# Softmax attention: the second pair of score matmuls between the two halves of the weighted values

## The chip, the cores and the metric

The kernel runs on one core of one Trainium2 chip. The metric is the device time of one execution in microseconds (us); the median over repeated runs counts. The engines are TensorE (PE; PEld is its weight load), VectorE (DVE), ScalarE (ACT), GpSimd (POOL) and SyncE (SP).

## The reference, cut to what matters

Two decoder layers over x of 16 sequences x 128 tokens x 128 features. Layer 0 is a self attention, a cross attention over ctx_1024 and a butterfly feed-forward; layer 1 is a linear attention, an autocorrelation attention and a mixture of experts. The change touches only the two softmax attentions of layer 0, both with 16 heads of 8 features:

```python
q = (x @ Wq).reshape(n, s, H, DH)
k = (x @ Wk).reshape(n, s, H, DH)
v = (x @ Wv).reshape(n, s, H, DH)
attn = jnp.einsum('nqhd,nkhd->nqkh', q, k) * scale
attn = jax.nn.softmax(attn, axis=-2)
z = jnp.einsum('nqkh,nkhd->nqhd', attn, v).reshape(n, s, d)
z = jnp.einsum('nqd,de->nqe', z, Wout)
return x + z
```

The cross attention is the same with the queries from x, keys and values straight from ctx_1024, and a bias on the output.

## The kernel before, in words

`attention` (L149) runs both attentions in one software pipeline of 32 passes, one pass for one sequence of one attention: passes 0 to 15 are the self attention, 16 to 31 the cross attention. The 16 heads of a sequence are four groups of four. Each engine has its own program; there is no scheduler: the order of an engine's instructions is the order of the code, and semaphores join the engines.

For one sequence the work is: first scores in bf16 (L569, one matmul of 512 columns per group, its four heads side by side), the negated row maximum of each head by VectorE (L473, one reduction per group), the maxima spread as a first term into a PSUM bank (L582, four matmuls per group) and the exact scores in fp32 added to it (L588), the exponential by ScalarE (L413, one per group), the weighted values in fp32 with a column of ones that gives the denominator (L608, 16 matmuls with an output of 32 partitions each, which are 32 matmul instructions in the trace, since the trace shows two for each of these fp32 matmuls), a copy out of PSUM by ScalarE (L419), transposes back (L620), division by VectorE (L479, L481), a transpose (L612), again the copy L419, the output projection (L624) and the residual (L490).

TensorE's loop (L640 to L652) works on several sequences at once. In pass i it does, in this order: the exact scores of sequence i (`shifted_scores`); the weighted values of sequence i-1 and the transpose of the divided output of i-2 (`values`); the first scores of groups 2 and 3 of sequence i+1 (`scores(i + 1, 1)`); the maxima of i+1 for groups 0 and 1; the transposes and the projection of `mix`; in 14 of the passes 1 to 30 (1 to 10, 13, 17, 21 and 25) a round of projections or transposes for a coming group of four sequences (`fill`, L545 to L554); the maxima for groups 2 and 3; the first scores of groups 0 and 1 of i+2.

What ties this order to other engines:

- The first scores use two banks for four groups, so those of groups 2 and 3 wait until VectorE has read groups 0 and 1 (`maxed`, L567).
- The maxima of group g of sequence i+1 wait for two things: the exponential of group g of sequence i, which frees the bank (`exped`, L578), and the reduction of group g of i+1 (`maxed`, L579).
- ScalarE's order in a pass is the exponentials of groups 0 and 1, `copy_mix` (L419), the exponentials of groups 2 and 3 (L441 to L446). `copy_mix` waits for `pv_done`, which `values` raises on its last instruction (L614); `mix` waits for `copy_mix` (L617).

Of the kernel before, what the change touches and what calls it, by code (L numbers as in the profile page):

```python
# [22 lines left out]
T = 128  # L23
D = 128
EPS = 1e-5
G, J = 4, 4
# [108 lines left out]
Q = 4  # L135
K_SLOTS = 3
GROUPS = B // Q
# [4 lines left out]
def bf16_head(ap):  # L142

    *lead, n = ap.shape
    wide = ap.bitcast(BF16)
    return wide[(slice(None),) * len(lead) + (slice(1, 2 * n, 2),)]


def attention(core, m, f, lin, a):  # L149
# [26 lines left out]
    bank_t, bank_s, bank_o, bank_r = core.bank[0:4], core.bank[4:6], core.bank[6], core.bank[7]  # L176
    scale = float(DH) ** -0.5
    SELF, CROSS = range(GROUPS), range(GROUPS, 2 * GROUPS)
# [10 lines left out]
    done_after = {kg: r + 1 for r, kg in enumerate(rounds)}  # L189

    def round_bank(r):
        return (bank_r, *bank_t[0:3])[r] if r < Q else bank_r
# [14 lines left out]
    def queries(s, g):  # L207
        return m.q[rows(g), s // Q % 2, s % Q, :]

    def keys(s, g):  # L210
        return m.k_j[rows(g), s % K_SLOTS, :, :] if s < B else m.k_ctx[rows(g), s - B, :, :]

    with nc.Block() as block:
# [321 lines left out]
        @block.tensor  # L535
        def _(pe):
            def fill(r):
                kind, g = rounds[r]
                bank = round_bank(r)
                if kind == "n" or g in CROSS:  # L540
                    if r >= Q:
                        pe.wait_ge(copied, 1 if r == Q else r)
                    pe.wait_ge(normed, Q * (g + 1))
                    for i in range(Q):
                        mm = pe.transpose(bank[:, i * T:(i + 1) * T], m.n[:, g % 2, i, :], core.ident[:, :])  # L545
                else:
                    pe.wait_ge(copied, r if r > Q else 1)
                    if kind == "v":
                        for i in range(Q):
                            mm = pe.matmul(bank[:, i * D:(i + 1) * D], m.nT[:, i * T:(i + 1) * T], m.wv[:, :],  # L550
                                           start=True, stop=True)
                    else:
                        mm = pe.matmul(bank[:, :], (m.wk if kind == "k" else m.wq)[:, :], m.nT[:, :],
                                       start=True, stop=True)  # L554
                mm.then_inc(filled, 1)

            def scores(s, pair):
                if s >= V:
                    return
                if pair == 0:  # L560
                    pe.wait_ge(copied, done_after["q", s // Q])
                    if s < B:
                        pe.wait_ge(k_made, s + 1)
                    elif s == B:
                        pe.wait_ge(k_ctx_in, 16)
                if s or pair:
                    pe.wait_ge(maxed, G * s + 2 * pair)  # L567
                for g in (2 * pair, 2 * pair + 1):
                    pe.matmul(bank_s[g % 2][:, :], bf16_head(queries(s, g)),  # L569
                              bf16_head(keys(s, g).rearrange("p j t -> p (j t)")), start=True, stop=True)\  # L570
                        .then_inc(scored, 1)

            def maxima(s, groups):
                if s >= V:
                    return
                for g in groups:
                    if s:
                        pe.wait_ge(exped, G * (s - 1) + g + 1)  # L578
                    pe.wait_ge(maxed, G * s + g + 1)  # L579
                    for j in range(J):  # L580
                        h = J * g + j
                        pe.matmul(bank_t[g][:, j * T:(j + 1) * T], m.nmax[:, h:h + 1].to_broadcast([T, T]),  # L582
                                  core.ident_b[:, :], start=(j == 0), stop=False, skip_group_check=True)

            def shifted_scores(s):
                for j in range(J):
                    for g in range(G):
                        mm = pe.matmul(bank_t[g][:, j * T:(j + 1) * T], keys(s, g)[:, j, :], queries(s, g),  # L588
                                       start=False, stop=(j == J - 1), skip_group_check=True)
                        if j == J - 1:  # L590
                            mm.then_inc(shifted, 1)

            def values(i):
                if i >= 2:
                    pe.wait_ge(o_done, i - 1)
                if i >= 3:
                    pe.wait_ge(x_done, i - 2)
                s = i - 1
                if s < V:
                    g = s // Q  # L600
                    pe.wait_ge(exped, G * (s + 1))
                    if s % Q == 0:
                        pe.wait_ge(*((copied, done_after["v", g]) if g in SELF else (v_made, g - GROUPS + 1)))
                    for half in range(2):
                        for odd in range(2):
                            for c in range(4):
                                h = 8 * half + 2 * c + odd
                                mm = pe.matmul(bank_o[32 * c:32 * c + 32, half * T:half * T + T],  # L608
                                               m.v[:, g % 2, s % Q, h, :], m.p[:, s % 2, h, :],
                                               start=(odd == 0), stop=(odd == 1), skip_group_check=True)  # L610
                if i >= 2:
                    mm = pe.transpose(bank_o[:, 2 * T:3 * T], m.o[:, :, :].rearrange("p h d -> p (h d)"),  # L612
                                      core.ident[:, :])
                mm.then_inc(pv_done, 1)  # L614

            def mix(i):
                pe.wait_ge(mix_copied, i)  # L617
                if i - 1 < V:
                    for half in range(2):
                        mm = pe.transpose(bank_o[:, half * T:half * T + T], m.mix[:, half, :], core.ident[:, :])  # L620
                if i >= 2:
                    if i == 2:
                        pe.wait_ge(out_in, 32)
                    mm = pe.matmul(bank_o[:, 2 * T:3 * T], m.mix[:, 2, :], m.w_out[(i - 2) // B][:, :],  # L624
                                   start=True, stop=True)
                mm.then_inc(mixed, 1)

            pe.wait_ge(ident_in, 16)
            fill(0)
            pe.wait_ge(proj_in, 48)  # L630
            for r in range(1, Q):
                fill(r)
            scores(0, 0)
            fill(Q)
            scores(0, 1)
            pe.wait_ge(copied, Q)
            pe.wait_ge(made, 4)
            maxima(0, range(G))
            scores(1, 0)
            for i in range(V + 2):  # L640
                if i < V:
                    shifted_scores(i)
                if i >= 1:
                    values(i)
                scores(i + 1, 1)
                maxima(i + 1, (0, 1))
                if i >= 1:
                    mix(i)
                if i in round_at:
                    fill(round_at[i])  # L650
                maxima(i + 1, (2, 3))
                scores(i + 2, 0)  # L652
# [1450 lines left out]
```

## Time and profile before

| what | value |
|---|---|
| time, median of 3 runs | 612.64 us (612.61, 612.64, 618.45) |
| the profiled execution's own time | 617.73 us |
| its span, first to last instruction | 615.6 us |
| mean granted clock of TensorE over the span | 0.875 |
| the 32 passes: first exact scores of pass 0 to those of pass 31 | 22.36 to 175.38 us |

The profile is of one execution. All durations come from it. In rows of a timeline the columns are the start in us, the duration in us from the first start to the last end of the instructions that the row merges, the engine, the line, the operation, the tiles written and read, the shapes and the count; idle time of the engine before it stands in brackets with what ended it.

### The profile page before, as it was taken

How to read it: one execution, taken by the hardware profiler on the slowest of the kernel's cores; microseconds unless marked ns; L12 is line 12 of the kernel's file. 1: busy time of each engine (PE TensorE's matmuls, PEld its weight loads, DVE VectorE, ACT ScalarE, POOL GpSimd, SP SyncE). 2: the span in 40 equal slices, each digit the busy share in tenths (PEclk: the TensorE clock that was granted, in tenths of full speed). 3: DMA queues.
4: the chain of work that ended last, by engine and by line, in shares of the span. 5: the costliest groups of instructions: out<-in, count | busy, mean ns of one | idle time of the engine just before them, and what ended most of it. 6: DMA issues, size and time to landing. Idle time of an engine off the chain costs nothing. (4 is left out here: it accounts for less than half of the span.)

```text
span 615.6 us, 13186 instructions
## 1 busy us (share of the span) xinstructions
PE 485.4 (79%) x4975; PEld 383.4 (62%) x4975; DVE 345.1 (56%) x934; ACT 239.0 (39%) x514; POOL 209.2 (34%) x234
## 2 busy tenths in 40 slices
PE   3879999999977979999999997996275232399960
PEld 1567777777754767888888886875155221266640
DVE  6546777777653446667766764344783767211114
ACT  3756666666542325444543541221121000132313
POOL 3546777799132233000000002123621000447750
PEclk9799999999996989999999997997585555599995
DMA  8960312200000011000000001200006000324417
GB/s 234 394 260 4 113 64 73 68 4 2 4 1 1 0 36 44 1 0 0 0 0 0 0 0 25 63 17 0 1 7 199 1 0 0 94 63 126 121 33 205
DMA packets 31460, 34.71 MB, mean 56 GB/s; under 512 B 5561, under 2 KB 25078, under 8 KB 31288
## 3 DMA queue, kind: packets, MB, share of 16 engines
q1 hardware_dynamic: 29208, 29.50, 15.3%
q0 software_dynamic: 2064, 4.60, 2.3%
q8 instruction: 31, 0.51, 0.4%
q14 instruction: 13, 0.11, 0.1%
q10 hardware_dynamic: 144, 0.00, 0.0%
HBM read 28.65 MB, written 5.46 MB: 55 GB/s over the span
## 5 line engine op out<-in xcount | busy, mean ns | idle before, releaser
L473 DVE TENSOR_REDUCE at_nmax<-bank 128x4 bf16<-128x512 f32 x128 | 82.5, 686 | 48.1 <-PE bank L569 48.1
L413 ACT ACTIVATE at_p<-bank 128x512 f32<-128x512 f32 x128 | 69.3, 597 | 38.2 <-PE bank L588 38.2
L95 POOL TENSOR_TENSOR var<-var,eps 128x12 f32<-128x12 f32 (+1 forms) x8 | 1.7, 206 | 191.1 <-DVE var L88 191.1
L1869 POOL DMA_INDIRECT mo_rows<-mo_n_rows,mo_src_row x24 | 23.0, 959 | 71.2 <-POOLq L1577 64.2
L582 PE MATMUL bank<-ident_b,at_nmax 128*128 128x128 bf16 x512 | 42.9, 222 | 3.9 <-DVE at_nmax L473 3.4
L582 PEld LDWEIGHTS bank<-ident_b,at_nmax 128*128 128x128 bf16 x512 | 31.0, 98 | 18.8 <-issue 9.5
L608 PE MATMUL bank<-at_p,at_v 128*32 128x128 f32 x1024 | 35.0, 276 | 3.9 <-issue 3.0
L1942 ACT ACTIVATE mo_h<-bank,mo_b 128x308 f32<-128x308 f32 x32 | 16.5, 517 | 47.1 <-PE bank L1905 47.1
L1913 PE MATMUL bank<-mo_w,mo_h 128*128 128x128 f32 (+1 forms) x192 | 32.9, 294 | 1.3 <-ACT mo_h L1942 1.3
L1040 PE MATMUL bank<-li_phi_q,li_phi_k 128*128 128x256 f32 x128 | 31.9, 393 | 0.9 <-DVE li_phi_q L908 0.9
L1051 PEld LDWEIGHTS bank<-li_v,li_am 128*128 128x128 f32 x256 | 29.8, 192 | 3.7 <-DVE li_am L915 3.1
L1051 PE MATMUL bank<-li_v,li_am 128*128 128x65 f32 x256 | 31.7, 277 | 0.1
L1913 PEld LDWEIGHTS bank<-mo_w,mo_h 128*128 128x128 f32 (+1 forms) x192 | 24.0, 172 | 11.9 <-ACT mo_h L1942 5.3
L608 PEld LDWEIGHTS bank<-at_p,at_v 128*32 128x32 f32 x1024 | 26.2, 110 | 8.1 <-issue 3.3
L1961 DVE COPY mo_xT<-bank 128x308 f32<-128x308 f32 x8 | 3.8, 478 | 48.2 <-PE bank L1896 48.2
L1637 PE MATMUL bank<-ro_reached,ro_ones_b 128*128 128x56 bf16 x160 | 10.9, 228 | 24.0 <-DVE ro_reached L1733 24.0
L1877 POOL DMA_INDIRECT mo_planes<-mo_y,mo_dst_row x24 | 23.7, 986 | 16.9 <-DVE mo_y L1968 10.5
L282 POOL TENSOR_TENSOR at_k_j<-at_kT,at_mask 128x512 f32<-128x512 f32 x16 | 16.6, 1039 | 30.7 <-PE bank L588 27.5
L1040 PEld LDWEIGHTS bank<-li_phi_q,li_phi_k 128*128 128x128 f32 x128 | 23.0, 190 | 4.3 <-DVE li_phi_q L908 1.1
L1002 ACT ACTIVATE li_tanh<-bank,li_gate_bias 128x128 f32<-128x128 f32 x64 | 18.2, 367 | 19.2 <-PE bank L1018 19.1
L989 ACT ACTIVATE li_clip_k<-bank 128x512 f32<-128x512 f32 x16 | 9.6, 597 | 40.3 <-PE bank L1018 40.3
L1637 PEld LDWEIGHTS bank<-ro_reached,ro_ones_b 128*128 128x128 bf16 x160 | 8.2, 121 | 26.7 <-DVE ro_reached L1733 25.4
(279 smaller groups left out, 1214.5 us busy)
## 6 DMA issues: line engine op xcount, KB each, us to landing
fo_w<-in_up_stages SPq DMA_DIRECT2D x9, 512.0 KB, 9.3
fo_w<-in_down_stages SPq DMA_DIRECT2D x9, 512.0 KB, 4.7
at_k_ctx<-in_ctx_heads SPq DMA_DIRECT2D x1, 4096.0 KB, 21.5
mo_w<-in_L_ffn_W SPq DMA_DIRECT2D x16, 256.0 KB, 3.1
mo_planes<-ro_zeros POOLq DMA_DIRECT2D x1, 2048.0 KB, 9.1
mo_got<-mo_planes SPq DMA_DIRECT2D x8, 256.0 KB, 4.8
x<-in_x SPq DMA_DIRECT2D x4, 256.0 KB, 3.5
au_ctx<-in_ctx SPq DMA_DIRECT2D x4, 256.0 KB, 4.0
```

Of the source, the lines that this page charges most:

```text
L282: pool.tensor_tensor(m.k_j[:, s % K_SLOTS, :, :], over(m.kT[:, g % 2, s % Q, :], J), m.mask[:, :].unsqueeze(2).to_broadcast([D, J, T]), AL ...
L413: act.activation(m.p[:, s % 2, J * g:J * g + J, :], bank_t[g][:, :].rearrange("p (j t) -> p j t", j=J), ACT.Exp, scale=scale).then_inc(exp ...
L473: dve.tensor_reduce(m.nmax[:, J * g:J * g + J], bank_s[g % 2][:, :].rearrange("p (j t) -> p j t", j=J), AX.X, ALU.max, negate=True).then_i ...
L582: pe.matmul(bank_t[g][:, j * T:(j + 1) * T], m.nmax[:, h:h + 1].to_broadcast([T, T]), core.ident_b[:, :], start=(j == 0), stop=False, skip ...
L608: mm = pe.matmul(bank_o[32 * c:32 * c + 32, half * T:half * T + T], m.v[:, g % 2, s % Q, h, :], m.p[:, s % 2, h, :], start=(odd == 0), sto ...
L1002: ins = act.activation(tanh[:, c, :], bank_g[:, c * T:(c + 1) * T], ACT.Tanh, bias=m.gate_bias[:, c:c + 1], scale=0.5)
L1040: mm = pe.matmul(bank_a[c // 2][:, 256 * (c % 2):256 * (c % 2) + 256], phi_k[:, c, :], phi_q[:, c, :, :].rearrange("p r t -> p (r t)"), st ...
L1051: mm = pe.matmul(bank_num[h // half][:, i * V1:(i + 1) * V1], am[:, h, :], v[:, h, :], start=True, stop=True)
L1637: mm = pe.matmul(bank_c[:, 0:TRIALS * E6], ones_b[:, :], reached[:, b, :, :].rearrange("t j e -> t (j e)"), start=(b == 0), stop=(b == B - 1))
L1869: pool.indirect_dma_start(out=rows[0:m, e % 2, r, :], out_offset=None, in_=n_rows, in_offset=bass.IndirectOffsetOnAxis(ap=src_row[0:m, til ...
L1877: pool.indirect_dma_start(out=planes, out_offset=bass.IndirectOffsetOnAxis(ap=dst_row[0:m, tile:tile + 1], axis=0), in_=y[0:m, e % 2, r, : ...
L1913: mm = pe.matmul(bank_y[r][0:m, 0:D], h[:, c, at[r]:at[r] + m], w2[:, par, c, :], start=(c == 0), stop=(c == CH6 - 1))
```

## The change

`values` takes a second argument and does one half of its matmuls per call; the two waits for the buffers, the wait for the exponentials and the wait for the values stand before the first half, the transpose and `pv_done` behind the second. In the loop the first scores of groups 2 and 3 stand between the two calls. Lines below `values` move down by one to five (L608 becomes L609, L612 L615, L620 L623, L624 L627). The other engines' programs keep their instructions and their order.

```diff
-            def values(i):
-                if i >= 2:
-                    pe.wait_ge(o_done, i - 1)
...
+            def values(i, half):
+                if half == 0:
+                    if i >= 2:
+                        pe.wait_ge(o_done, i - 1)
...
-                    for half in range(2):
-                        for odd in range(2):
...
+                    for odd in range(2):
+                        for c in range(4):
+                            h = 8 * half + 2 * c + odd
+                            mm = pe.matmul(bank_o[32 * c:32 * c + 32, half * T:half * T + T],
+                                           m.v[:, g % 2, s % Q, h, :], m.p[:, s % 2, h, :],
+                                           start=(odd == 0), stop=(odd == 1), skip_group_check=True)
+                if half == 0:
+                    return
...
                 if i >= 1:
-                    values(i)
+                    values(i, 0)
                 scores(i + 1, 1)
+                if i >= 1:
+                    values(i, 1)
                 maxima(i + 1, (0, 1))
```

TensorE in a pass of the cross attention without a fill, from the exact scores to the transposes of `mix`, before (at_v and at_p are values and exponentials, at_k_ctx and at_q keys and queries, at_nmax the negated maxima, at_o the divided output, at_mix what `copy_mix` wrote):

```order
L588 MATMUL bank<-at_q,at_k_ctx 128x128 x16
L608 MATMUL bank<-at_p,at_v 32x128 [waits at_exped,at_x_done,at_o_done]
L608 MATMUL bank<-at_p,at_v 32x128 x15
L612 MATMUL bank<-ident,at_o 128x128
L569 MATMUL bank<-at_k_ctx,at_q 128x512 [waits at_maxed]
L569 MATMUL bank<-at_k_ctx,at_q 128x512
L582 MATMUL bank<-ident_b,at_nmax 128x128 [waits at_maxed,at_exped]
...
L620 MATMUL bank<-ident,at_mix 128x128 [waits at_mix_copied]
```

and the same place now:

```order
L588 MATMUL bank<-at_q,at_k_ctx 128x128 x16
L609 MATMUL bank<-at_p,at_v 32x128 [waits at_exped,at_x_done,at_o_done]
L609 MATMUL bank<-at_p,at_v 32x128 x7
L569 MATMUL bank<-at_k_ctx,at_q 128x512 [waits at_maxed]
L569 MATMUL bank<-at_k_ctx,at_q 128x512
L609 MATMUL bank<-at_p,at_v 32x128 x8
L615 MATMUL bank<-ident,at_o 128x128
L582 MATMUL bank<-ident_b,at_nmax 128x128 [waits at_maxed,at_exped]
...
L623 MATMUL bank<-ident,at_mix 128x128 [waits at_mix_copied]
```

The two score matmuls, with their wait for at_maxed, moved up past the transpose and eight of the matmuls of the values; the transpose, on which `pv_done` hangs, now stands behind them.

ScalarE in the same passes, which has the same rows before and now (at_p the exponentials, at_mix the copy):

```order
L413 ACTIVATE at_p<-bank 128x512 [waits at_pv_done,at_shifted]
L413 ACTIVATE at_p<-bank 128x512 [waits at_shifted]
L419 ACTIVATE at_mix<-bank 128x384 [waits at_pv_done]
L413 ACTIVATE at_p<-bank 128x512 [waits at_shifted] x2
L385 ACTIVATE at_n<-x,at_shift,rstd 128x128
```

Nothing moved here: the copy still stands between the second and the third exponential.

## Rows read from the trace of the kernel before

**Rows 1.** The page's first part: busy time of each engine over the span.

```profile
PE 485.4 (79%) x4975; PEld 383.4 (62%) x4975; DVE 345.1 (56%) x934; ACT 239.0 (39%) x514; POOL 209.2 (34%) x234
```

**Rows 2.** Waits in 105 to 163 us: waiter, releaser, us in total, times, longest.

```profile
ACT at_p L413 <- PE bank L588: 18.8, 13, 1.9
...
PE bank L582 <- DVE at_nmax L473: 2.1, 10, 0.2
```

**Rows 3.** Timeline of pass 16, a pass without a fill.

```profile
105.17 1.27 PE L588 MATMUL bank<-at_q,at_k_ctx 32*128 32x128 f32 x32
105.59 1.29 DVE L473 TENSOR_REDUCE at_nmax<-bank 128x4 bf16<-128x512 f32 x2 [0.21 <-PE bank L569]
...
106.38 1.08 PE L608 MATMUL bank<-at_p,at_v 128*32 128x128 f32 x32
106.48 1.09 ACT L413 ACTIVATE at_p<-bank 128x512 f32<-128x512 f32 x2 [1.56 <-PE bank L588]
...
107.39 0.33 PE L612 MATMUL bank<-ident,at_o 128*128 128x128 f32 x1
...
107.65 0.40 PE L569 MATMUL bank<-at_k_ctx,at_q 32*128 32x512 bf16 x2
107.76 0.49 ACT L419 ACTIVATE at_mix<-bank 128x384 f32<-128x384 f32 x1 [0.19 <-PE bank L612]
...
107.98 0.62 PE L582 MATMUL bank<-ident_b,at_nmax 128*128 128x128 bf16 x8
108.08 1.29 DVE L473 TENSOR_REDUCE at_nmax<-bank 128x4 bf16<-128x512 f32 x2 [1.00 <-PE bank L569]
108.14 1.08 ACT L413 ACTIVATE at_p<-bank 128x512 f32<-128x512 f32 x2
...
108.44 0.39 PE L620 MATMUL bank<-ident,at_mix 128*128 128x128 f32 x2
...
109.52 0.38 PE L582 MATMUL bank<-ident_b,at_nmax 128*128 128x128 bf16 x4 [0.21 <-DVE at_nmax L473]
...
109.78 0.28 DVE L490 TENSOR_TENSOR x<-bank,x 128x128 f32<-128x128 f32 x1
...
109.85 1.27 PE L588 MATMUL bank<-at_q,at_k_ctx 32*128 32x128 f32 x32
```

**Rows 4.** Groups by line: the mean duration of one values matmul is the second number.

```profile
L608 PE MATMUL bank<-at_p,at_v 128*32 128x128 f32 x1024 | 35.0, 276 | 3.9 <-issue 3.0
```

**Rows 5.** Timeline of pass 9, a pass with a fill.

```profile
74.72 0.39 PE L620 MATMUL bank<-ident,at_mix 128*128 128x128 f32 x2
...
75.17 1.02 PE L553 MATMUL bank<-at_nT,at_wq 128*128 128x512 f32 x2
...
76.04 0.61 PE L582 MATMUL bank<-ident_b,at_nmax 128*128 128x128 bf16 x8
```

**Rows 6.** Timeline of pass 31, where the transposes of mix wait for the copy.

```profile
177.86 0.49 ACT L419 ACTIVATE at_mix<-bank 128x384 f32<-128x384 f32 x1 [0.20 <-PE bank L612]
...
178.40 0.44 PE L620 MATMUL bank<-ident,at_mix 128*128 128x128 f32 x2 [0.58 <-ACT at_mix L419]
...
178.68 0.39 PE L624 MATMUL bank<-at_w_out,at_mix 128*128 128x128 f32 x2
```

**Rows 7.** Timeline of pass 15, where VectorE has variances before the reductions.

```profile
100.43 0.28 DVE L490 TENSOR_TENSOR x<-bank,x 128x128 f32<-128x128 f32 x1
...
101.31 1.28 DVE L473 TENSOR_REDUCE at_nmax<-bank 128x4 bf16<-128x512 f32 x2
```

**Rows 8.** Timeline of pass 3: TensorE stands still inside the values.

```profile
43.35 0.42 PE L608 MATMUL bank<-at_p,at_v 128*32 128x128 f32 x6 [3.00 <-issue]
```

**Rows 9.** Stretches: length, busy us and count of PE, PEld, DVE, ACT, POOL; granted clock; DMA.

```profile
39.00:44.00 5.00, 2.00 (x49) 1.29 (x41) 1.00 (x3) 1.08 (x2) 3.75 (x5) 1.00 0.65 230
...
105.17:175.38 70.21, 67.64 (x1348) 53.83 (x1347) 51.96 (x128) 43.50 (x87) 45.14 (x31) 1.00 0.07 18
```

More of the change, by code:

```diff
@@ L591, in shifted_scores @@
                             mm.then_inc(shifted, 1)
-            def values(i):
-                if i >= 2:
-                    pe.wait_ge(o_done, i - 1)
-                if i >= 3:
-                    pe.wait_ge(x_done, i - 2)
+            def values(i, half):
+                if half == 0:
+                    if i >= 2:
+                        pe.wait_ge(o_done, i - 1)
+                    if i >= 3:
+                        pe.wait_ge(x_done, i - 2)
                 s = i - 1
@@ L600, in values @@
                     g = s // Q
-                    pe.wait_ge(exped, G * (s + 1))
-                    if s % Q == 0:
-                        pe.wait_ge(*((copied, done_after["v", g]) if g in SELF else (v_made, g - GROUPS + 1)))
-                    for half in range(2):
-                        for odd in range(2):
[L606 to L610, printed above, removed]
+                    if half == 0:
+                        pe.wait_ge(exped, G * (s + 1))
+                        if s % Q == 0:
+                            pe.wait_ge(*((copied, done_after["v", g]) if g in SELF else (v_made, g - GROUPS + 1)))
+                    for odd in range(2):
[4 more added lines that the diff above has]
+                                           start=(odd == 0), stop=(odd == 1), skip_group_check=True)
+                if half == 0:
+                    return
                 if i >= 2:
```

## The prediction

> **What bounds the kernel now.** The page's first part comes first: TensorE is busy for 79% of the span, VectorE 56%, ScalarE 39% [rows 1]. That share mixes seven stages, so the stretch that the change touches is read alone, in the waits of the cross attention and then in the timeline of one pass. The waits [rows 2] show TensorE stopped by VectorE's reductions ten times in 13 passes, 0.2 us each, 2.1 us together: once in each of the ten passes without a fill. ScalarE waits much longer for the exact scores (18.8 us), but that only says that it has time to spare somewhere in the pass; where it has none must be seen in the timeline.
>
> The reader should lay rows 3 out by engine. One pass runs from the exact scores at 105.17 to the next at 109.85, 4.68 us, and TensorE fills it but for one hole of 0.21 us, before the maxima of group 3 at 109.52. Those need two things: the last reduction, which ends at 108.08 + 1.29 = 109.37, and the last exponential, which ends at 108.14 + 1.08 = 109.22. VectorE is the later one by 0.15 us. But ScalarE ends almost as late, and for a reason of its own: after its first two exponentials it runs the copy of the mix, in order, and the copy waits for the transpose L612, which ends at 107.39 + 0.33 = 107.72; it starts at 107.76, and the last two exponentials, whose scores have lain ready since 105.17 + 1.27 = 106.44, run behind it. So there are two loops through TensorE of nearly one length: first scores of groups 2 and 3 → reductions → maxima of group 3, and values → transpose L612 → copy → two exponentials → maxima of group 3. The change shortens the first and lengthens the second.
>
> **The change part by part.** It adds no arithmetic. It moves two matmuls and their wait, per pass, past the transpose and half of the values, in passes 1 to 30 (pass 0 has no values, pass 31 no next sequence).
>
> *The first scores come earlier.* They start at 107.65 now. The values start at 106.38 and take 1.08: 32 instructions of 276 ns each [rows 4], in eight sets of four side by side, so (1.08 - 0.30)/7 = 0.11 from set to set, taking 0.30 for the first; half of them is 0.30 + 3 x 0.11 = 0.63. What follows another kind of matmul starts 0.07 before that one's end (107.39 against 107.46, 107.65 against 107.72, 107.98 against 108.05 [rows 3]). So the scores could start 0.56 after the values, at 106.94. Their wait is for the reductions of groups 0 and 1, which end at 105.59 + 1.29 = 106.88, so it costs 0 to 0.1 us; I take 0, since the margin is 0.06 and a release with a single wait took 0.05 (below). The reductions of groups 2 and 3 then end about 0.7 us earlier than now, and the hole of 0.21 us goes.
>
> *The transpose comes later.* The scores hold TensorE 0.33 us (107.65 to 107.98), and the second half pays its own start and end: values start + 0.56 + 0.33 + 0.56 = 1.45 against 107.39 - 106.38 = 1.01 now. The transpose is late by 0.44, and with it the copy (107.76 → 108.20) and the last two exponentials (ending 109.22 → 109.66). TensorE's own total hardly moves: now it goes values, transpose, scores, maxima, with three changes of the matmul's kind; afterwards values, scores, values, transpose, maxima, again three, since transpose and maxima are both 128 x 128.
>
> *Passes without a fill, 16 of 30.* The maxima of group 3 have to wait for the last exponential. From copy to L620 a release with a single wait took 177.86 + 0.49 = 178.35 to 178.40, 0.05 us [rows 6]. As things are, ScalarE would release them at 109.22 + 0.05 = 109.27, 0.25 before they start. Of the 0.44 that is added, 0.25 is therefore paid by the vanished hole, and 0.19 remains; I take 0.22, since the order of two waits in one place can cost some hundredths more. 16 x 0.22 = 3.5 us.
>
> *Passes with a fill, 14 of 30.* Here the fill stands between the transposes of mix and the second maxima [rows 5]: 75.17 to 76.04 is 0.87 us in which both reductions and exponentials end, so there is no hole to win. But the transposes L620 stand in front of the fill and wait for the copy. Now the copy ends at 108.25 and L620 starts at 108.44 without a wait; afterwards the copy ends at 108.69, L620 starts at 108.74, 0.30 later. After such a wait the next matmuls came 178.68 - 178.40 = 0.28 later [rows 6] instead of 108.66 - 108.44 = 0.22, which the rows of pass 9 bear out in sum: 75.17 - 74.72 = 0.45 for L620 and L624 together. So 0.30 + 0.06 = 0.36, rounded up by the drift above to 0.37: 14 x 0.37 = 5.2 us. Nothing covers it, since everything behind it on TensorE is queued in order.
>
> *Two passes with variances ahead of the reductions.* VectorE finishes the residual and then computes variances before the first reductions of the next pass; in pass 15 the reductions start 101.31 - 100.43 = 0.88 after the residual [rows 7], against 105.59 + 4.68 - 109.78 = 0.49 in rows 3, and they end 0.39 later in the pass. That hid behind the values before; now the moved scores wait for it in full view, and the transpose behind them. The longer pass takes about 0.1 off. 2 x 0.3 = 0.6 us (passes 15 and 19).
>
> *The start.* In pass 3 TensorE stands still for 3.00 us with nothing to wait for in the program [rows 8], while the DMA share is 0.65 [rows 9]. If that stall ends with the DMA traffic and not so long after its beginning, what passes 1 and 2 lose is hidden by it. Bounds 0 and -1.1 (three passes); I take -0.8, two passes of 0.37 and a bit of the third.
>
> *Sum:* 3.5 + 5.2 + 0.6 - 0.8 = +8.5 us. The profiled execution took 617.73 us, 2.1 more than its span of 615.6; it would become 626.2. It lies 5.1 us above the median of 612.64, and the three runs themselves differ by that much, so the change is put on the median: 612.64 + 8.5 = 621.1 us, 1.4% slower. A measurement of this kernel can tell about 1% from no change, here 6 us.
>
> **A rule to weigh.** Rows 3 show that TensorE starts a matmul of another shape only when the one before it is nearly done. The Trainium skill, "TensorEngine Tiling (Array Packing)", Key Properties, says that changing the tiling mode, and not just the tile, drains the array. The trace agrees for the pairs that it has (0.07 us before the end, three times); it has no first scores behind values. By the rule the moved scores cannot run beside the values, and the delay of 0.44 stands; without it they could run beside the second half, which is the second rival below.
>
> **The rivals.**
>
> 1. *The wait on the copy doesn't bind.* If the copy came back in time for L620, the fill passes would lose nothing and the gain or loss would be that of the other passes: 612.64 + 3.5 + 0.6 = 616.7. For it: now L620 has 108.44 - 108.25 = 0.19 of margin. Against it: the transpose is 0.44 late, more than twice that. It decides where the transpose is less than about 0.15 late.
> 2. *Faster: the scores run beside the second half of the values.* Exact scores do start 0.01 to 0.02 us behind first scores, since both use 32 rows of the array. If the values let the scores in beside them, the transpose would hardly move, the hole would go, and the maxima of group 3 would follow the last exponential: 16 x 0.25 = 4.0 us won, 608.6. Against it: every change of shape in rows 3 costs its 0.33 or 0.20 in order. It turns into a gain from the point where the transpose is late by less than 0.15 to 0.2.
> 3. *The scores themselves wait.* If the release of the moved scores takes as long as that of the maxima does now (109.37 to 109.52, 0.15), they start at 107.03, 0.09 late, in every pass, and if the reductions of groups 0 and 1 are pushed back as well, by up to 0.2: 30 x 0.09 to 0.2 = 2.7 to 6 us more, 623.8 to 627.1. For it: the margin is only 0.06. Against it: VectorE's residual ends at 110.06 in rows 3 while the next reductions wait for their scores until 110.27.
> 4. *The clock.* More holes in TensorE could lower its granted clock. Against it: in 39 to 44 us it was busy for 2.00 of 5.00 us and the clock stayed at 1.00, the 2.4 GHz level, as in the cross attention [rows 9]. At half of that the passes would cost over 100 us.
>
> **How the numbers follow.** Forecast (+5 to +11): 0.70. Rival 1: 0.12. Rival 2: 0.05. Rival 3: 0.11. Rival 4: 0.01, and 0.01 that something else wins. Slower by over 1% (above 618.8) are rivals 3 and 4 and about nine tenths of the forecast, 0.75; within 1% are rival 1, over half of rival 2 (0.03) and the rest of the forecast, 0.22; faster by over 1% (below 606.5) the other 0.02 of rival 2, if it wins more than its price, and the 0.01, 0.03. For the range I go down to 615, which takes in most of rival 1 and a start that hides all of its 1.1, and up to 628, rival 3 or one of the longer executions that the runs of before also show.
>
> **What would show it.** In the profile after: passes without a fill of about 4.90 us instead of 4.68 and those with a fill longer by 0.37; the hole before the maxima of group 3 put down to ScalarE's exponentials instead of the reductions; a new hole of about 0.3 us before the transposes of mix, put down to the copy; VectorE's second wait in the pass (1.00) much shorter; ScalarE's wait for the transpose (0.19) at 0.6 or more. The prediction is wrong if the copy starts less than 0.2 us later behind the values' start than now, if the passes with a fill keep their length, or if the hole before group 3 goes and nothing takes its place.

## The result, and the profile after

The changed kernel takes 622.95 us (median of 17 runs, 618.87 to 628.78), the kernel before 614.06 us in the 17 runs beside it. The ratio is 1.012, with a 95% interval of 1.0088 to 1.0152: slower by 1.2%. The ratio leaves out one disturbed run of the changed kernel (628.78 us) and equals the quotient of the means of the others (622.76 and 615.37 us, 7.4 us apart); the medians lie 8.9 us apart. Forecast was 1.4%, 621.1 us. The profiled execution has a span of 622.2 us, against 615.6 us before.

The page's first part after, to lay beside [rows 1], and the group of the values, beside [rows 4]:

```profile
PE 492.5 (79%) x4975; PEld 382.2 (61%) x4975; DVE 347.8 (56%) x934; ACT 239.1 (38%) x514; POOL 209.1 (34%) x234
...
L609 PE MATMUL bank<-at_p,at_v 128*32 128x128 f32 x1024 | 40.8, 278 | 0.9 <-DVE x L490 0.9
```

Only TensorE's busy time has moved much, by 7.1 us, with the same instructions. Most of it is the values: 40.8 us instead of 35.0, since two runs of 0.64 us stand in a pass for one of 1.08. Whether that is the loss, or only where it can be seen, the page can't tell.

The same pass as [rows 3], pass 16, in the timeline of the changed kernel:

```profile
107.17 1.27 PE L588 MATMUL bank<-at_q,at_k_ctx 32*128 32x128 f32 x32
107.58 1.29 DVE L473 TENSOR_REDUCE at_nmax<-bank 128x4 bf16<-128x512 f32 x2 [0.26 <-PE bank L569]
...
108.37 0.64 PE L609 MATMUL bank<-at_p,at_v 128*32 128x128 f32 x16
...
108.95 0.40 PE L569 MATMUL bank<-at_k_ctx,at_q 32*128 32x512 bf16 x2
...
109.28 0.65 PE L609 MATMUL bank<-at_p,at_v 128*32 128x128 f32 x16
109.38 1.29 DVE L473 TENSOR_REDUCE at_nmax<-bank 128x4 bf16<-128x512 f32 x2 [0.31 <-PE bank L569]
...
109.85 0.33 PE L615 MATMUL bank<-ident,at_o 128*128 128x128 f32 x1
...
110.01 0.61 PE L582 MATMUL bank<-ident_b,at_nmax 128*128 128x128 bf16 x8
110.22 0.49 ACT L419 ACTIVATE at_mix<-bank 128x384 f32<-128x384 f32 x1 [0.66 <-PE bank L615]
110.60 1.08 ACT L413 ACTIVATE at_p<-bank 128x512 f32<-128x512 f32 x2
110.76 0.20 PEld L623 LDWEIGHTS bank<-ident,at_mix 128*128 128x128 f32 x2 [0.31 <-ACT at_mix L419]
...
111.73 0.23 PEld L582 LDWEIGHTS bank<-ident_b,at_nmax 128*128 128x128 bf16 x4 [0.26 <-ACT at_p L413]
...
112.08 1.27 PE L588 MATMUL bank<-at_q,at_k_ctx 32*128 32x128 f32 x32
```

Read from the start of the values at 108.37. VectorE got what it was meant to get: its second pair of reductions starts 1.01 us after the values (109.38), not 1.70 (108.08 - 106.38 in [rows 3]), and its wait fell from 1.00 to 0.31 us. But the transpose starts 1.48 us after them instead of 1.01, and the copy 1.85 instead of 1.38. The last exponential now ends at 110.60 + 1.08 = 111.68 and the weights for the maxima of group 3 follow at 111.73, released by ScalarE. Ahead of them stands a new wait, 0.31 us, of the mix on the copy. The pass is 4.92 us long (112.08 - 107.17 = 4.91 in these rounded rows) instead of 4.68.

The waits, over 105 to 163 us as in [rows 2]:

```profile
ACT at_mix L419 <- PE bank L615: 8.5, 12, 1.0
...
PEld bank L623 <- ACT at_mix L419: 3.7, 12, 0.3
...
PEld bank L569 <- DVE at_nmax L473: 2.5, 11, 0.5
PEld bank L615 <- issue: 2.4, 12, 0.2
PEld bank L582 <- ACT at_p L413: 2.4, 9, 0.3
```

The row in which TensorE waits for VectorE before the maxima is gone. In its place TensorE's weight loads (PEld) wait in every pass for the copy. The last row, nine waits for the exponentials, needs care: the waits of the kernel before have one like it,

```profile
PEld bank L582 <- ACT at_p L413: 3.2, 9, 0.4
```

and the timeline of pass 16 before puts the load for group 3 down to ScalarE as well:

```profile
109.49 0.24 PEld L582 LDWEIGHTS bank<-ident_b,at_nmax 128*128 128x128 bf16 x4 [0.36 <-ACT at_p L413]
```

So the name alone shows nothing; the times do. Before, this load came 0.27 us after the last exponential had ended (109.22) and 0.12 after the last reduction (109.37). Now it comes 0.05 after the last exponential (111.68 to 111.73), and the reductions have been done since 109.38 + 1.29 = 110.67.

Pass 9, with a fill, as in [rows 5]; it begins at the first row, the next pass at the last, which the end of the window cuts short:

```profile
71.04 1.27 PE L588 MATMUL bank<-at_q,at_k_j 32*128 32x128 f32 x32
...
74.09 0.49 ACT L419 ACTIVATE at_mix<-bank 128x384 f32<-128x384 f32 x1 [0.66 <-PE bank L615]
...
74.63 0.44 PE L623 MATMUL bank<-ident,at_mix 128*128 128x128 f32 x2
...
75.13 1.02 PE L553 MATMUL bank<-at_nT,at_wq 128*128 128x512 f32 x2
...
75.99 0.61 PE L582 MATMUL bank<-ident_b,at_nmax 128*128 128x128 bf16 x8
...
76.55 0.71 PE L588 MATMUL bank<-at_q,at_k_j 32*128 32x128 f32 x12
```

It takes 5.51 us against 5.13 before. From mix to fill it is 0.50 us instead of 0.45, and the mix itself starts 0.05 us after the copy has ended (74.58): the copy sets it.

### The profile page after: what moved, and what is told of

Its sections match the earlier page's. It is cut to its first block and busy times, and to the rows that moved or that the text cites. A ratio compares the mean times of both kernels' runs of the same rounds, so it can differ in the third digit from the quotient of the medians.

```text
span 622.2 us, 13186 instructions
## 1 busy us (share of the span) xinstructions
PE 492.5 (79%) x4975; PEld 382.2 (61%) x4975; DVE 347.8 (56%) x934; ACT 239.1 (38%) x514; POOL 209.1 (34%) x234
## 5 line engine op out<-in xcount | busy, mean ns | idle before, releaser
L582 PEld LDWEIGHTS bank<-ident_b,at_nmax 128*128 128x128 bf16 x512 | 34.6, 102 | 11.4 <-ACT at_p L413 7.0
L609 PE MATMUL bank<-at_p,at_v 128*32 128x128 f32 x1024 | 40.8, 278 | 0.9 <-DVE x L490 0.9
L609 PEld LDWEIGHTS bank<-at_p,at_v 128*32 128x32 f32 x1024 | 24.2, 109 | 11.9 <-issue 7.1
L419 ACT ACTIVATE at_mix<-bank 128x384 f32<-128x384 f32 (+2 forms) x33 | 15.9, 481 | 24.3 <-PE bank L615 23.9
```

## The experiments

Each kernel was run beside the kernel before. The lengths of passes are differences between starts of L588 in each run's timeline; passes of one kind repeat to 0.01 us within a run, but for passes 6, 10 and 30 (0.02 to 0.04 us off) and those named below. "4 to 31" is the time from pass 4 to pass 31. It leaves out the start, where TensorE's stalls and its clock differ from execution to execution, and all that comes from pass 31 on, which took 435.6 to 442.8 us in the eight profiled executions.

| kernel | without a fill (pass 23) | with projections (pass 9) | with transposes (pass 21) | 4 to 31 | against before | ratio of times, 95% interval |
|---|---|---|---|---|---|---|
| before | 4.68 | 5.13 | 4.71 | 129.19 | | |
| changed | 4.92 | 5.51 | 5.08 | 137.84 | +8.65 | 1.012 (1.0088 to 1.0152) |
| e1 | 4.65 | 5.51 | 5.09 | 134.06 | +4.87 | 1.0096 (1.0065 to 1.0127) |
| e2 | 4.92 | 5.21 | 4.92 | 136.49 | +7.30 | 1.0106 (1.0063 to 1.0149) |
| e3 | 4.65 | 5.21 | 4.74 | 131.71 | +2.52 | 1.0034 (1.0006 to 1.0062) |
| e4 | 4.78 | 5.37 | 4.95 | 133.50 | +4.31 | 1.0085 (1.0047 to 1.0124) |
| f1 | 4.51 | 5.07 | 4.60 | 126.26 | -2.93 | 0.9962 (0.9941 to 0.9982) |
| f2 | 4.68 | 5.24 | 4.81 | 130.34 | +1.15 | 1.0031 (1.0007 to 1.0055) |

**e1: the copy behind the third exponential**, in the changed kernel.

```diff
-                    if g == 1 and i >= 1:
+                    if g == 2 and i >= 1:
                         copy_mix(i)
```

> The changed kernel with one edit on ScalarE: the copy of the mix stands behind the third exponential instead of behind the second. Theory (the late transpose holds the copy, and the copy holds the last two exponentials in ScalarE's order): the last exponential ends 2.83 us after the start of the values instead of 3.31, the maxima of group 3 follow those of group 2 at once, and a pass without a fill falls from 4.92 us to 4.64 to 4.68; a pass with a fill keeps its 5.51 (5.09 with transposes), since there the copy itself, not the exponentials, is waited for. About 4.3 us less than the changed kernel, so some 4.6 us (0.75%) above the kernel before. Rival (TensorE is the bound and pays for the second break in the values): 4.92 stays, and the time is that of the changed kernel, 1.2 to 1.4% above before.

The timeline of a pass without a fill:

```profile
108.64 0.64 PE L609 MATMUL bank<-at_p,at_v 128*32 128x128 f32 x16
108.75 1.57 ACT L413 ACTIVATE at_p<-bank 128x512 f32<-128x512 f32 x3 [1.55 <-PE bank L588]
...
110.49 0.49 ACT L419 ACTIVATE at_mix<-bank 128x384 f32<-128x384 f32 x1 [0.16 <-PE bank L615]
...
110.87 0.59 ACT L413 ACTIVATE at_p<-bank 128x512 f32<-128x512 f32 x1
111.03 0.44 PE L623 MATMUL bank<-ident,at_mix 128*128 128x128 f32 x2
...
111.53 0.61 PE L582 MATMUL bank<-ident_b,at_nmax 128*128 128x128 bf16 x8
```

The copy starts 1.85 us after the values, exactly as late as in the changed kernel, and TensorE does all that it did there; only one exponential has gone ahead of the copy. The eight maxima now run in one piece of 0.61 us, and the pass falls from 4.92 to 4.65. Passes with a fill keep 5.51 and 5.09. So in a pass without a fill the loss was ScalarE's order behind the late transpose: the break in the values is still there, and the pass is no longer than before (4.65 against 4.68). What the break costs TensorE is read from e3 and f1 below. One thing was missed: passes 15 and 19 keep 5.23 us, since they wait for variances, so passes 4 to 31 fall by 3.8 us and not by 4.3. The whole time is 0.96% above before, with 0.75% expected; its interval does not separate e1 from the changed kernel, its pass lengths do.

**e2: the fill before the mix**, in the changed kernel.

```diff
+                if i in round_at:
+                    fill(round_at[i])
                 if i >= 1:
                     mix(i)
-                if i in round_at:
-                    fill(round_at[i])
```

> The changed kernel with one edit on TensorE: the fill stands before the transposes and the projection of the mix instead of behind them. Theory (in the passes with a fill the whole loss is the wait of the mix on the late copy): the 0.87 us of a fill cover that wait, and a pass with a fill falls from 5.51 to 5.13 to 5.18 us (from 5.09 to 4.71 to 4.76 with transposes); passes without a fill keep 4.92. About 5 us less than the changed kernel, some 4 us (0.6%) above before. Rival (the second break in the values costs TensorE time of its own): the passes with a fill keep 5.4 or more.

Passes with projections fall to 5.21, as the theory has it, though not quite to 5.13. Two things were missed. Passes with transposes stop at 4.92, because a fill of 0.45 us hides the wait for the copy but then the maxima of group 3 wait for the exponentials, as in a pass without a fill. And passes 7 and 11 take 5.51, since the mix is now late, VectorE's division with it, and the variances that follow in passes 6 and 10 push the reductions behind TensorE. Passes 4 to 31 get back 1.35 us where about 5 were expected. In pass 7 the moved scores wait for the reductions:

```profile
60.05 1.28 DVE L473 TENSOR_REDUCE at_nmax<-bank 128x4 bf16<-128x512 f32 x2
60.22 0.64 PE L609 MATMUL bank<-at_p,at_v 128*32 128x128 f32 x16
...
61.39 0.40 PE L569 MATMUL bank<-at_k_j,at_q 32*128 32x512 bf16 x2 [0.52 <-DVE at_nmax L473]
```

The interval of e2 does not separate it from the changed kernel; its pass lengths do.

**e3: both edits together.**

> The changed kernel with both edits, the copy behind the third exponential and the fill before the mix. Theory: both losses go, passes without a fill 4.64 to 4.68 us, with a fill 5.13 to 5.18; the time is that of the kernel before within 0.3%, with two passes of 0.3 us more each where variances delay the reductions. Rival (TensorE pays for the break): at least half of the 1.2% stays.

4.65, 5.21 and 4.74 us: both losses are gone but for 0.08 us in passes with projections and the four passes that wait for variances (5.23 us in 11, 15 and 19, 5.32 in 7). These four carry 2.3 of the 2.52 us that are left in passes 4 to 31; two of them were expected, with 0.3 us each. In place of 1.2%, 0.34% is left, just outside the 0.3% that was expected. The rival's half, some 4.3 us, is not in the pass lengths; the interval of the whole time, which reaches 0.62%, would not exclude it by itself.

**e4: a smaller move**, from the kernel before: the scores pass the transpose only.

```diff
                 if i >= 1:
-                    values(i)
+                    values(i, 0)
                 scores(i + 1, 1)
+                if i >= 1:
+                    values(i, 1)
```

Here `values(i, 0)` holds all 16 matmuls of the values and `values(i, 1)` the transpose alone.

> The kernel before with a smaller move: the first scores of groups 2 and 3 go past the transpose of the divided output only, and all of the weighted values stay in one piece. Theory: the transpose is late by 0.33 us instead of 0.47, so a pass without a fill takes 0.33 less the 0.25 of ScalarE's margin more, 4.76 to 4.80 us, and one with a fill 5.34 to 5.40 (4.92 to 4.98 with transposes): about 5 us (0.8%) above before. Rival (the break of the values into two halves is what costs): no loss, and the hole of 0.21 us goes, 4.47 to 4.55 us in a pass without a fill, 5.13 with one, 3 us below before.

```profile
140.66 1.08 PE L614 MATMUL bank<-at_p,at_v 128*32 128x128 f32 x32
...
141.68 0.40 PE L569 MATMUL bank<-at_k_ctx,at_q 32*128 32x512 bf16 x2
142.01 0.33 PE L596 MATMUL bank<-ident,at_o 128*128 128x128 f32 x1
142.11 1.29 DVE L473 TENSOR_REDUCE at_nmax<-bank 128x4 bf16<-128x512 f32 x2 [0.74 <-PE bank L569]
142.17 0.61 PE L582 MATMUL bank<-ident_b,at_nmax 128*128 128x128 bf16 x8
142.37 0.49 ACT L419 ACTIVATE at_mix<-bank 128x384 f32<-128x384 f32 x1 [0.52 <-PE bank L596]
```

The transpose is 142.01 - 140.66 = 1.35 us behind the values, 0.34 late, with the values in one piece, and all three kinds of pass grow as the theory says: 4.78, 5.37, 4.95. The loss follows the lateness of the transpose (0.34 costs 0.10 and 0.24; 0.47 costs 0.24 and 0.38), and the rival, no loss without the break, falls. The break has its part in the changed kernel, the 0.13 by which it makes the transpose later still. Passes 15 and 19 are as long as the others here: the scores come late enough for the variances.

**f1: e4's order with both edits.**

> The order of the run before (first scores of groups 2 and 3 past the transpose only, the values in one piece), with the copy of the mix behind the third exponential and the fill before the mix. Theory: the reductions start 0.25 us earlier than in the kernel before, the copy that is 0.33 late no longer holds the last but one exponential nor a fill, and TensorE saves a change of the matmul's shape, since the transpose and the maxima follow each other: passes without a fill 4.50 to 4.56 us against 4.68 before, with a fill 5.05 to 5.10 against 5.13 (4.58 to 4.64 with transposes against 4.71). About 3.5 us (0.6%) below the kernel before. Rival (moving those scores up can't pay, whatever the order around them): as before or slower, 4.65 us or more in a pass without a fill.

```profile
104.06 1.29 DVE L473 TENSOR_REDUCE at_nmax<-bank 128x4 bf16<-128x512 f32 x2 [0.74 <-PE bank L569]
...
104.32 0.49 ACT L419 ACTIVATE at_mix<-bank 128x384 f32<-128x384 f32 x1
104.71 0.59 ACT L413 ACTIVATE at_p<-bank 128x512 f32<-128x512 f32 x1
104.86 0.20 PEld L624 LDWEIGHTS bank<-ident,at_mix 128*128 128x128 f32 x2 [0.31 <-ACT at_mix L419]
...
105.36 0.61 PE L582 MATMUL bank<-ident_b,at_nmax 128*128 128x128 bf16 x8
...
106.34 1.29 DVE L473 TENSOR_REDUCE at_nmax<-bank 128x4 bf16<-128x512 f32 x2
```

4.51, 5.07 and 4.60 us, each where it was expected, and the time is below that of both kernels: 0.38% under before, with the interval clear of 1. It is less than the 0.6% forecast; the four passes with variances ahead take 0.15 more than their like (4.75 in 7, 4.66 in 11, 15 and 19), and 2.93 us is all that passes 4 to 31 give. The mix still waits 0.31 us for the copy, and the first reductions start as VectorE's residual ends, without a wait for their scores (106.34): VectorE has nothing to spare at that place, though it still waits 0.74 us for the moved scores (104.06).

Two comparisons say what each part is worth. e3 and f1 differ only in whether the scores break the values, and every kind of pass is 0.14 us shorter without the break (4.65 to 4.51, 5.21 to 5.07, 4.74 to 4.60). So TensorE does pay for the break; in the passes of e1 and e3 without a fill the vanished hole covers that price. In a pass without a fill, f2 (next) and f1 differ only in the moved scores: 4.68 against 4.51, so the smaller move is worth 0.17 us there once the copy stands behind the third exponential. The kernel before with both edits was not run, so in passes with a fill the share of the fill's new place stays open.

**f2: the kernel before with the copy behind the third exponential.**

> The kernel before with one edit on ScalarE: the copy of the mix behind the third exponential. Theory: in the kernel before the maxima of group 3 wait for VectorE's last reduction, not for ScalarE, so the passes keep 4.68 and 5.13 us and the time is that of before within 0.3%. Rival (ScalarE's order bounds the kernel before as well): 4.47 to 4.6 us in a pass without a fill, 1.5 to 3 us less.

The end of pass 16:

```profile
105.45 1.29 DVE L473 TENSOR_REDUCE at_nmax<-bank 128x4 bf16<-128x512 f32 x2 [1.00 <-PE bank L569]
105.67 0.63 ACT L413 ACTIVATE at_p<-bank 128x512 f32<-128x512 f32 x1
...
106.86 0.24 PEld L582 LDWEIGHTS bank<-ident_b,at_nmax 128*128 128x128 bf16 x4 [0.28 <-issue]
```

4.68 stays. The last exponential now ends 0.56 us before the load for group 3 (106.30 to 106.86) instead of 0.27, and the load still comes 0.12 after the last reduction (106.74), as before: in the kernel before ScalarE's order was not the bound, VectorE's was. The passes with a fill were expected to keep their length and lost 0.10 us each, since the copy now ends later than TensorE comes to the mix. The 0.3% is slower, barely clear of 1.

## Why the prediction was right

*The time.* Passes 4 to 31 carry +8.65 us; the steps put the same passes at 16 x 0.22 + 11 x 0.37 + 0.6 = 8.2. What is missing there is 0.02 us in a pass without a fill and 0.01 in one with a fill. Medians differ by 8.9 us, means by 7.4; the forecast was 8.5. That the total comes so close is in part luck, since it holds a term for the start that no run shows (below).

*The scores come earlier, at little cost: right.* They start 0.58 us after the values (0.56 forecast), and the values go on 0.33 us later. Rival 3's wait costs next to nothing there: the weight load of the moved scores stops 0.2 us for VectorE in a pass (2.5 us in 11 waits above), but the load of the transpose, which waits for no other engine, stops as long behind the second half (2.4 in 12), and both halves hold TensorE alike (0.58 and 0.57).

*The transpose comes later: right, a bit short.* 0.47 us instead of 0.44. Each half of the values is a little longer than was worked out from the merged row: 0.64 and 0.65 us instead of 0.63, and what follows starts 0.58 and 0.57 after its start instead of 0.56.

*Passes without a fill: right.* 4.92 - 4.68 = 0.24 us, with 0.22 forecast. That this is the last exponential's doing, e1 shows. The working had 0.44 - 0.25 = 0.19 and put 0.03 on top for two waits in one place; what came on top was the 0.03 by which the transpose is later, and 0.02 behind the release. So the size is right, the reason for its last 0.03 is not.

*Passes with a fill: right.* 0.38 us with 0.37 forecast, and the copy's doing, as e2 shows for the passes with projections, which get back 0.30 of it, and e3 against e1 for those with transposes (5.09 to 4.74).

*Two passes with variances: right.* Passes 15 and 19 take 5.23 us, 0.31 more than their neighbours, with 0.3 forecast; in pass 15 the moved scores wait 0.25 us for VectorE, against none in the passes around:

```profile
104.03 0.40 PE L569 MATMUL bank<-at_k_ctx,at_q 32*128 32x512 bf16 x2 [0.25 <-DVE at_nmax L473]
```

*The start: the step that no run bears out.* The -0.8 rested on a stall of 3.00 us in one execution. In the profiled execution of the changed kernel pass 3 takes 5.09 us and has no such stall; nor has it in f2, where TensorE's order is that of before (4.82). The first pass is the longer one instead (6.70 against 5.18 us), but not by a stall: from 22 to 28 us the granted clock was 0.50, the 1.2 GHz level, in that execution and on average 0.76 in the one of before. In both it had fallen before the first pass began, ahead of anything that the change moves. Stalls and clock of the start differ between executions, so nothing can be said of what they hide. Without the term the forecast would have been 9.3; the interval of the ratio, 5.4 to 9.3 us, does not tell the two apart.

*The rivals.* The copy binds, so the first falls. The second, scores beside the values, falls with 108.95, 109.28: the second half begins only 0.33 us after the scores, as their like did before the maxima. The clock was at 1.00 from 29 to 176 us in both traces; in the first pass it was lower, as told above. Of the changed kernel (columns as in [rows 9]):

```profile
105.00:176.00 71.00, 67.72 (x1272) 50.78 (x1272) 50.61 (x120) 42.36 (x86) 46.51 (x32) 1.00 0.06 18
```

## What to carry to other kernels

When two engines' loops through a third are nearly of one length, moving work forward for one moves it back for the other: write down, for every instruction that is jumped over, who waits for it and what is queued behind that waiter, before counting the gain. Here the instruction jumped over released a copy on an engine that works in order, with two ready exponentials behind it. Where such a move is still wanted, first take the waiter out of the way (the copy one place later, the fill one place earlier): the change itself then loses 0.3% instead of 1.2% (e3), and the smaller move past the transpose alone wins 0.4% (f1) instead of losing 0.85% (e4). And the name of a releaser in the profile is to be checked against the times: the row that named ScalarE stood there before it was true.

## What the runs showed that was not expected

The transpose and the maxima behind it, both 128 x 128, follow each other after 0.16 us (109.85 to 110.01), where the transpose before first scores held TensorE for 0.26 [rows 3]. e4's order has it too, with no break in the values: from the start of the values to the maxima it takes 142.17 - 140.66 = 1.51 us, with the same instructions for which the kernel before takes 107.98 - 106.38 = 1.60. Having matmuls of one shape side by side goes with a gain of about 0.1 us a pass here. That f1's passes with a fill could fall below those of the kernel before (5.07 against 5.13) fits this, though no run tried it alone.
